# A routed feed-forward kernel on one core: row-number products moved between the first slot's two half-picks, slot words moved from VectorE to GpSimd

## What is computed

```python
# conditioned layer: a dense matrix and a low-rank adapter chosen per batch
c = x @ W.T + ((x @ A[adapter].T) @ Bm[adapter].T) * scalings[adapter]
# router: integer softmax over 8 experts, the best two of a token, renormalised
logits = c @ w_gate.T
top_w, top_i = top_k(softmax_integer(logits), 2);  top_w /= top_w.sum(-1)
# experts of hidden size 704
for e in range(8):
    out += combine[:, e:e+1] * ((silu(c @ w1[e].T) * (c @ w3[e].T)) @ w2[e].T)
return x + out
```

## Time and profile before

| | us |
|---|---|
| median of 3 runs | 204.21 |
| lowest, highest | 203.08, 204.86 |
| profiled execution, its own time | 204.69 |
| profiled execution, span in the trace | 203.0 |
| outside the span | 1.69 |

### The profile page before, as it was taken

How to read it: one execution, slowest core, us unless ns; L and a number is a source line. 1 busy time by engine, 2 the same in 40 slices (tenths; PEclk the granted TensorE clock), 3 DMA queues, 4 the chain that set the end, 5 groups by cost and what they waited for, 6 DMA issues and landing times.

```text
span 203.0 us, 3879 instructions
## 1 busy us (share of the span) xinstructions
PE 192.1 (95%) x1209; PEld 169.2 (83%) x1209; DVE 108.7 (54%) x308; ACT 82.4 (41%) x224; POOL 129.7 (64%) x116
## 2 busy tenths in 40 slices
PE   7699999899998999999999999999999997999992
PEld 6387997788897899889988998899888886989881
DVE  0678899783646345334534453444675434435483
ACT  2576583368733143323332343233323323333560
POOL 8300004559899999999999999996345473316700
PEclk9999999999999999999999999999999999999999
DMA  5999320799996115283274383017212111110915
GB/s 134 408 368 361 136 103 19 232 301 385 349 396 235 57 55 155 61 284 75 88 258 126 90 260 113 0 16 275 74 55 53 53 55 61 43 55 26 346 73 208
DMA packets 14403, 32.67 MB, mean 161 GB/s; under 512 B 2384, under 2 KB 7632, under 8 KB 14256
## 3 DMA queue, kind: packets, MB, share of 16 engines
q1 hardware_dynamic: 10704, 25.17, 36.2%
q0 software_dynamic: 2128, 5.64, 8.8%
q10 hardware_dynamic: 1552, 1.61, 2.4%
HBM read 25.45 MB, written 6.96 MB: 160 GB/s over the span
## 4 chain that ended last, share of the span: by engine, by line
PE 80%; DVE 10%; DMA 5%; ACT 2%; issue 1%; SPq 0%; DVEq 0%
PE gu L1169 27%; PE gu L1178 14%; PE ya L1206 8%; PE ht L1185 7%; PE ya L1207 7%; PE ya L1208 6%; DMA x<-x_t 4%; DVE w_all L847 3%; PE xt L1149 2%; PE gu L1223 2%; DMA rows<-cond_rows,src_i 2%; PE ya L1201 1%; PE gu L1055 1%; PE ya L1200 1%; PE gu L1236 1%
## 5 line engine op out<-in xcount | busy, mean ns | idle before, releaser
L1169 PE MATMUL gu<-w_all,xs_hi 128*128 (+2 forms) x276 | 70.9, 378 | 0.1
L872 DVE TENSOR_TENSOR hid<-gu,sg 128x256 f32<-128x256 f32 x46 | 19.5, 425 | 65.8 <-ACT sg L611 62.5
L1169 PEld LDWEIGHTS gu<-w_all,xs_hi 128*128 128x128 f32 x276 | 46.8, 188 | 4.4 <-issue 0.3
L611 ACT ACTIVATE sg<-gu 128x256 f32<-128x256 f32 x46 | 17.7, 384 | 75.3 <-PE gu L1178 75.3
L458 POOL TENSOR_TENSOR w_all<-raw,w_all 128x1024 fp32r<-128x1024 f32 (+2 forms) x14 | 44.0, 3156 | 3.6 <-DVE w_all L860 3.5
L452 POOL DMA_INDIRECT rows<-cond_rows,src_i x22 | 23.6, 1073 | 30.5 <-DVE src_i L828 25.9
L1206 PE MATMUL ya<-w_all,h_hi 128*128 (+1 forms) x115 | 38.4, 334 | 2.4 <-DVE rows L893 2.3
L1178 PE MATMUL gu<-w_all,xs_lo 128*128 (+1 forms) x138 | 40.6, 375 | 0.0
L474 POOL DMA_INDIRECT expert_rows<-rows,dst_i x21 | 20.3, 969 | 26.3 <-DVE hid L872 14.5
L1207 PE MATMUL ya<-w_all,h_hi 128*128 (+1 forms) x115 | 32.5, 282 | 0.0
L1208 PE MATMUL ya<-w_all,h_lo 128*128 (+1 forms) x115 | 32.2, 280 | 0.0
(11 more groups left out here) (190 smaller groups left out, 261.1 us busy)
## 6 DMA issues: line engine op xcount, KB each, us to landing
raw<-expert_weights SPq DMA_DIRECT2D x6, 896.0 KB
raw<-expert_weights SPq DMA_DIRECT2D x6, 640.0 KB
raw<-expert_weights SPq DMA_DIRECT2D x6, 512.0 KB
expert_rows<-zeros SPq DMA_DIRECT2D x1, 2048.0 KB
rows<-expert_rows SPq DMA_DIRECT2D x4, 512.0 KB, 5.0
cond_rows<-c_rows ACTq DMA_DIRECT2D x4, 256.0 KB, 2.0
raw<-x_t SPq DMA_DIRECT2D x1, 1024.0 KB
out_t<-raw SPq DMA_DIRECT2D x4, 256.0 KB, 2.2
```

The source lines that it names most:

```text
L872: nc.vector.tensor_tensor(hid[i % HBUFS][:, :].rearrange("p (a b) -> p a b", b=P), bank[:, :].rearrange("p (a k b) -> p a k b", k=2, b=P)[ ...
L1169: nc.tensor.matmul(out, stay_hi[:, kc * P:(kc + 1) * P], moving(at, part + first + kc * P, n), start=kc == 0 and part == HI_COLS, stop=False)
```

## The change

It does four things.

1. The picks of slot 0 are cut in two calls, `first_rows(0)` and `first_rows(1)`, one for each half of 128 features, each with an increment of `xt_done` of its own. The 16 row-number products with their wait for `hot_ready` stand between them.
2. The halves go to two banks: the first to `xt`, the second to `ya` (`first_at`). ScalarE copies each half by itself (`first_hi`), VectorE takes the rest of each by itself (`first_slot_lo`). The counts that others wait for grow by one (`halves_of`).
3. On ScalarE `expert_hi(1, 2)` now stands between `first_hi(0)` and `first_hi(1)`; on VectorE `tokens_of_rows` stands between `first_slot_lo(0)` and `first_slot_lo(1)`. The first gate and up product waits for the half that it is about to use.
4. The ten instructions for the slot words leave VectorE. GpSimd makes the words with 15 instructions of its own, each waiting for the one before, from the moment at which VectorE has `base_of` and ahead of GpSimd's gathers.

```diff
+        first_at = [xt[:, 0:P], ya[:, 0:P]]
+        def halves_of(s):
+            return KC + s
...
-            sp.wait_ge(xt_done, 1)
+            sp.wait_ge(xt_done, halves_of(0))
             raw_weights(STAGED_LOW)
...
+            def then(ins):
+                words_made[0] += 1
+                ins.then_inc(word_step, 1)
+                pool.wait_ge(word_step, words_made[0])
+
+            pool.wait_ge(bases_ready, 1)
+            then(nc.gpsimd.tensor_scalar(ends[:, :], filled[:, :], 1.0, None, ALU.max))
+            then(nc.gpsimd.tensor_scalar(ended[:, :], base_of[:, :], 1.0 / P, None, ALU.mult))
+            then(nc.gpsimd.tensor_tensor(ends[:, :], ends[:, :], ended[:, :], ALU.add))
+            then(nc.gpsimd.tensor_copy(ends_i[:, :], ends[:, :]))
+            then(nc.gpsimd.tensor_tensor(at_slot[:, :, :], slot_no[:, :, :],
+                                         ends[0:1, :].unsqueeze(1).broadcast_to([1, SLOTS + 1, EXPERTS]),
+                                         ALU.subtract))
+            then(nc.gpsimd.tensor_scalar(at_slot[:, :, :], at_slot[:, :, :], 0.0, None, ALU.is_ge))
+            then(nc.gpsimd.tensor_tensor(at_slot[:, :, 0:4], at_slot[:, :, 0:4], at_slot[:, :, 4:8], ALU.add))
+            then(nc.gpsimd.tensor_tensor(at_slot[:, :, 0:2], at_slot[:, :, 0:2], at_slot[:, :, 2:4], ALU.add))
+            then(nc.gpsimd.tensor_tensor(slot_f[:, :], at_slot[:, :, 0], at_slot[:, :, 1], ALU.add))
+            then(nc.gpsimd.tensor_scalar(slot_f[:, :], slot_f[:, :], 1.0, float(EXPERTS), ALU.add, ALU.min))
+            then(nc.gpsimd.tensor_tensor(slot_w[:, :], slot_f[:, :], digits[:, :], ALU.mult))
+            by_word = slot_w[:, :].rearrange("p (w i) -> p w i", i=PER_WORD)
+            then(nc.gpsimd.tensor_tensor(by_word[:, :, 0:3], by_word[:, :, 0:3], by_word[:, :, 3:6], ALU.add))
+            then(nc.gpsimd.tensor_tensor(words_f[:, :], by_word[:, :, 0], by_word[:, :, 1], ALU.add))
+            then(nc.gpsimd.tensor_tensor(words_f[:, :], words_f[:, :], by_word[:, :, 2], ALU.add))
+            nc.gpsimd.tensor_copy(words[:, :], words_f[:, :]).then_inc(slots_ready, 1)
...
             expert_hi(1, 1)
-            expert_hi(1, 2)
...
+            def first_hi(kc):
+                act.wait_ge(xt_done, kc + 1)
+                cols = slice(kc * P, (kc + 1) * P)
+                copy(xs_hi[0][:, cols], first_at[kc]).then_inc(xs_hi_ready, 1)
...
-            slot_hi(0)
+            first_hi(0)
+            expert_hi(1, 2)
+            first_hi(1)
...
-            chain(nc.vector.tensor_reduce(base_of[:, :], based[:, :, :], AX_X, ALU.add))
+            nc.vector.tensor_reduce(base_of[:, :], based[:, :, :], AX_X, ALU.add).then_inc(bases_ready, 1)
+            dve.wait_ge(bases_ready, 1)
...
-            beside(nc.vector.scalar_tensor_tensor(ends[:, :], filled[:, :], 1.0, filled[:, :], ALU.max, ALU.max))
...
-            nc.vector.tensor_copy(words[:, :], words_f[:, :]).then_inc(slots_ready, 1)
...
-            slot_lo(0)
+            first_slot_lo(0)
             tokens_of_rows()
+            first_slot_lo(1)
...
+            def first_rows(kc):
                 for t in range(TILES):
                     pe.wait_ge(c_out, t // 2 + 1)
-                    last = nc.tensor.matmul(xt[:, kc * P:(kc + 1) * P], c_rows[:, t, kc * P:(kc + 1) * P],
+                    last = nc.tensor.matmul(first_at[kc], c_rows[:, t, kc * P:(kc + 1) * P],
                                             picks[:, t, :], start=t == 0, stop=t == TILES - 1)
-            last.then_inc(xt_done, 1)
+                last.then_inc(xt_done, 1)
+
+            pe.wait_ge(picks_ready, 1)
+            first_rows(0)
             pe.wait_ge(hot_ready, 1)
...
             last.then_inc(src_done, 1)
+            first_rows(1)
...
-                if j == 0:
-                    pe.wait_ge(xs_hi_ready, s + 1)
+                if j == 0 and s:
+                    pe.wait_ge(xs_hi_ready, halves_of(s))
...
                 for kc in range(KC):
+                    if i == 0:
+                        pe.wait_ge(xs_hi_ready, kc + 1)
...
-                    pe.wait_ge(xs_lo_ready, s + 1)
+                    pe.wait_ge(xs_lo_ready, halves_of(s))
```

More of the change, by code:

```diff
@@ L145, in moe_kernel @@
         ends = sb("ends", [P, EXPERTS])
+        ended = sb("ended", [P, EXPERTS])
         ends_i = sb("ends_i", [P, EXPERTS], I32)
@@ L273, in moe_kernel @@
         dst_ready = sem("dst_ready")
+        bases_ready = sem("bases_ready")
+        word_step = sem("word_step")
         slots_ready = sem("slots_ready")
@@ L449, in _ @@
                            allow_small_or_imprecise_dtypes=True).then_inc(consts_ready, 1)
+            words_made = [0]
+            def then(ins):
[21 more added lines that the diff above has]
+            nc.gpsimd.tensor_copy(words[:, :], words_f[:, :]).then_inc(slots_ready, 1)
             def gather(s):
@@ L619, in slot_hi @@
             def slot_hi(s):
-                act.wait_ge(xt_done, s + 1)
+                act.wait_ge(xt_done, halves_of(s))
                 copy(xs_hi[s % 2][:, :], xt[:, 0:DIM]).then_inc(xs_hi_ready, 1)
+            def first_hi(kc):
+                act.wait_ge(xt_done, kc + 1)
+                cols = slice(kc * P, (kc + 1) * P)
+                copy(xs_hi[0][:, cols], first_at[kc]).then_inc(xs_hi_ready, 1)
             def hidden_hi(i):
@@ L862, in slot_lo, with first_slot_lo @@
             def slot_lo(s):
-                dve.wait_ge(xs_hi_ready, s + 1)
+                dve.wait_ge(xs_hi_ready, halves_of(s))
                 nc.vector.tensor_tensor(xs_lo[s % 2][:, :], xt[:, 0:DIM],
                                         as_f32(xs_hi[s % 2][:, :]), ALU.subtract).then_inc(xs_lo_ready, 1)
+            def first_slot_lo(kc):
+                dve.wait_ge(xs_hi_ready, kc + 1)
+                cols = slice(kc * P, (kc + 1) * P)
+                nc.vector.tensor_tensor(xs_lo[0][:, cols], first_at[kc], as_f32(xs_hi[0][:, cols]),
+                                        ALU.subtract).then_inc(xs_lo_ready, 1)
             def hidden(i):
@@ L1128, in _ @@
             conditioned(3)
-            pe.wait_ge(picks_ready, 1)
-            for kc in range(KC):
+            def first_rows(kc):
                 for t in range(TILES):
                     pe.wait_ge(c_out, t // 2 + 1)
-                    last = nc.tensor.matmul(xt[:, kc * P:(kc + 1) * P], c_rows[:, t, kc * P:(kc + 1) * P],
+                    last = nc.tensor.matmul(first_at[kc], c_rows[:, t, kc * P:(kc + 1) * P],
                                             picks[:, t, :], start=t == 0, stop=t == TILES - 1)
-            last.then_inc(xt_done, 1)
+                last.then_inc(xt_done, 1)
+            pe.wait_ge(picks_ready, 1)
+            first_rows(0)
             pe.wait_ge(hot_ready, 1)
```

## The result

The changed kernel is **slower: 205.28 us against 204.26** (medians of 20 runs each), ratio 1.0054 with a 95% interval of 1.0036 to 1.0072. The forecast was 203.0, in a range from 201.6 to 204.6. The profiled execution took 205.78, its span 203.8.

What follows compares the result with a forecast made beforehand. TensorE, busy 192.1 of 203.0 us, was taken as the bound. Its 1.15 us idle before slot 1's transpose, less 0.1 for a new wait, plus 0.1 for a gap, rounded to 1.2: median 203.0 from 204.21, range 201.6 to 204.6.

Steps and rivals of the forecast that it cites:

- The words on GpSimd: GpSimd's 15 word instructions behind `base_of`: 5.3 us, from 23.0 to 28.3, costing nothing.
- the gather's 30.78: Start of the gather of slot 1's rows: 30.78 in place of 32.70, 1.92 us earlier.
- rival 4: GpSimd's words, ahead of the gathers, end past 32.7: slower than before, 207.1 at the upper row; chance 0.06.
- Rival 2: GpSimd and VectorE contend; GpSimd's columns hold VectorE up by at most 1.3 us: gain 0.7, 203.5; chance 0.05.
- row-number products: On TensorE, with 16 picks in front: from 28.10 to about 29.25, in place of 31.04.
- code: VectorE reads the row numbers in `tokens_of_rows`, now from 29.67 to 30.48, before from 31.59 to 32.40.
- gain at the transpose: TensorE's idle 1.15 us before slot 1's transpose is won, less 0.1 for a new wait: 1.05.
- new wait for the second half: Item 0 on TensorE waits for ScalarE's copy of the second half: 0 to 0.2 us, taken as 0.1.
- the gap in front of `gate_up(3)`: TensorE's gap of 0.10, laid to issue, just behind the removed wait, may close with it: 0.1 gained.
- 0.8 of margin: Gather lands at 34.31, TensorE is ready at 35.12: 0.8 us of the 1.92 are not used.
- Rival 1: Stalls laid to no engine, as near 168 us, fall elsewhere: 201.5 (chance 0.13) or 204.5 (chance 0.08).
- both parts are needed: Without the new order the products come at 31.04; without the shorter VectorE list code is read at 31.6.

Runs made afterwards that it cites:

- the kernel with the words given: The changed kernel with the slot words' computation left out, GpSimd writing them as constants in the start-up; ratio 0.9941 to the kernel before, median 203.37 us.

## Why the prediction was wrong

- **The step that failed is the one named "The words on GpSimd".** It took 5.3 us for the 15 instructions and called them covered by the gather's 30.78. Alone they take 5.45, so the estimate of their own length was good. Beside VectorE they take 9.90. From there it is the mechanism of rival 4: they end past the point at which the gather used to start. I had held the memsets of four numbers against it and had given it 0.06. They were the wrong yardstick: they have no input, as the words' instructions do. In the trace of before they even ran beside a VectorE instruction with two SBUF inputs, and all six were over in 0.26. That the missing input is the reason was not tried.

```profile
6.17 0.26 POOL L446 MEMSET digits<- 1x4 f32 x6
...
6.19 0.43 DVE L690 TENSOR_TENSOR pk_lo<-pack,pk_hi 128x256 fp32r<-128x256 f32 x1 [6.19 <-ACT pk_hi L553]
```

- **Rival 2 had the cause and the wrong sufferer.** I let GpSimd's few columns hold VectorE up, by their own number. The traces show mostly the reverse: a GpSimd instruction of 48 columns that begins beside VectorE's instruction of 1280 columns ends only behind it. VectorE lost about 0.6 us in all (`hot_r` 0.40, the low parts 0.2), GpSimd 4.45. The rule cited from the Trainium skill (GPSIMD Engine Reference, Key points), that the engines contend when VectorE has two SBUF inputs, agrees with the traces: L474 is 1.56 beside `hot_r` and 0.69 without it, L475 1.96 and 0.38.
- **The other terms held**, shown by the kernel with the words given: row-number products 5.35 behind `base_of` (forecast 28.10, +5.33), code at +6.91 (+6.90), gather at +8.03 (+8.01), gain at the transpose 1.09 (1.05) and the same 1.09 behind `ya`. The new wait for the second half was 0.17, taken as 0.1. The 0.1 that I added for the gap in front of `gate_up(3)` didn't come: 0.18 us are idle there, before 0.10. In the changed kernel itself the code was read at +7.41, half a microsecond late through VectorE's own share of the contention; that alone would have fitted into the 0.8 of margin.
- **The size.** The gather starts 0.95 later than before and slot 1's transpose comes 0.83 later; behind `ya` it is 0.99, as the gap in front of `gate_up(3)` is 0.27 in place of 0.10, and the medians differ by 1.0. Against the kernel with the words given the transpose is 1.92 late. The length of the words alone is worth 1.1 of this, the whole forecast gain: where only the words moved, they end at the same place and the transpose comes at +13.55. The other 0.8, which makes the changed kernel slower than before and not equal to it, is the later start and landing of its gather behind the words. Its cause was not shown. Rival 1, the stall near 168 us, isn't in the profile after, whose part behind the `ya` wait is 1.2 us shorter (157.43 against 158.64); in the eight others with that wait in the table it is 157.1 to 157.8. So it looks like one of the profiled execution of before that doesn't tell in the medians: with the words back on VectorE the three places in the table are within 0.13 of before, no such stall is in the profile, and the times agree (1.0007).
- That both parts are needed, and that behind `base_of` only the rows' arrival counts until slot 1, was right and is shown by the two kernels with one part each and by the two with words given.

## What to carry over

An engine's idle time is not free room if the neighbour streams two SBUF operands there: look at what the other engine runs in that window before moving small work into it, and price each small GpSimd instruction with an input at what is left of the VectorE instruction that is under way when it begins (for L474 and L483 the next one came on top). If such work must go there, put it into the stretch before the large instructions, and keep it out of the queue ahead of a DMA issue that TensorE waits for. Work that isn't urgent is better put behind the urgent instruction on its own engine than in front of it on another.

## What was not expected of the hardware

- GpSimd instructions on one partition and 48 to 192 columns, alone 0.26 to 0.69 us, took 1.40 to 1.96 beside VectorE instructions of 384 to 2048 columns with two SBUF inputs, and ended within about 0.25 us behind the end of one of these. Even an add of four numbers took 0.94 beside one of 256 and one of 512 columns, 0.19 alone.
- The one that began first lost little: L471 took 0.71 (0.59 alone) with `hot_r` beginning behind it, and `hot_r` (128x2048, 16-bit) took the loss.
- VectorE's `hot_r` went from 1.22 to 1.62 us beside GpSimd, `tok_s` from 0.36 to 0.38, the two low parts from 3.41 to 3.62.
- The record of the first gather's issue on GpSimd was 1.2 us or 1.6 to 1.9, in step with whether a VectorE instruction of 256 or 512 columns with two SBUF inputs was under way when it began.
